# One 128-column product per pair of batches split into two 64-column products, one for each batch

## The chip, the cores and the metric

The kernel runs on one core of a Trainium2 chip. The time is the device time of one execution in microseconds (us). TensorE multiplies (a weight load, LDWEIGHTS, and then a matmul that streams the other operand's columns past it), VectorE and ScalarE read PSUM and write SBUF, GpSimd copies between places of SBUF, and SyncE issues most of the DMAs. The profile calls them PE (with PEld for the weight loads), DVE, ACT, POOL and SP.

## The reference, cut to what matters

64 batches of 64 tokens by 512 features go through four residual layers. The first two have a dense part and a low-rank adapter that is chosen per batch; the last two mix the 64 tokens of a batch with a 64 by 64 matrix chosen per batch.

```
x = x + x @ W_base.T + ((x @ Wt.T) @ A0[e0].T @ B0[e0].T) @ Wp.T * s0[e0]   # rank 16, 4 adapters
x = x + x @ W1.T + (x @ A1[e1].T) @ B1[e1].T * s1[e1]                       # rank 16, 8 adapters
x = x + einsum('bct,bcd->bdt', x, W2[e2])      # mixes tokens
x = x + einsum('bct,bcd->bdt', x, W3[e3])      # mixes tokens
```

## The kernel before

The first 48 us make tables out of the weights. With the identities added, the two dense layers become one 512 by 512 matrix G, kept as a high and a low part (`g01`, both in the 4-byte type fp32r, which the matmul reads at reduced precision; two parts win the precision back). The adapters become, for each adapter e, 16 columns U (`u_tab`, high and low part) and 16 rows V (`v_table`, in DRAM).

Then come 32 steps, one for each pair of batches, in 8 turns of 4 (`QUADS`, `QUAD`; the 6 turns in the middle are a hardware loop). A pair is 128 rows: 64 tokens of batch 0 and 64 of batch 1. TensorE does in one step (`step`, line 816):

- `mix` for the next pair: y = x^T times the token matrix, 4 full fp32 matmuls, which the profile shows as 8 records of 128 weight columns and 128 streamed columns. ScalarE copies the high part yh out of PSUM (`high_y`, line 402) and VectorE makes the low part yl (`low_y`, line 578), both into `yy`.
- z for this pair: 4 matmuls, one for each 128 of the 512 features. The weights are the 128 columns [Uh | Ul], 64 and 64, and each 64 are (batch 0, layer 1), (batch 0, layer 2), (batch 1, layer 1), (batch 1, layer 2) with 16 each. The streamed operand is [yh | yl] of both batches, 256 columns. Of the 128 by 256 results in `z_ps` only those are used where batch meets batch.
- in the third step of a turn (u = 2, seven times in all) `token_mix`, 16 records of 64 by 64, makes the token matrices of the next turn; ScalarE copies them (`copy_p`).
- o for this pair: 12 matmuls of yh and yl with G, 512 streamed columns, into one bank of `o_ps`, and behind them 2 matmuls with `z` as weights and V as streamed operand. Only these 2 wait for z.

Out of `z_ps` the kernel makes Uh·yh (rounded, to `z` rows 0 to 63: ScalarE, two instructions, one a batch), then its rounding rest plus Ul·yh plus Uh·yl (to `z` rows 64 to 127: `low_z` on VectorE, line 586, three stages of two instructions). `z` is zero where batch does not meet batch. ScalarE's order in a step is: z, (`copy_p` if u = 2), `high_y` of the next pair, `double_v` (line 421) of the next pair, `copy_out` (line 430) of this one. VectorE's is `low_z`, `low_y` of the next pair, and in the first two steps of a turn `add_w3` and `place_w2` (lines 606 and 621) for the next turn. GpSimd's `place_u` (line 313) fills `u_sel`, the weights of z, two steps ahead, once the z matmuls that read it are done. All engines run their orders as written and meet in semaphores: `z_done`, `zh_set`, `zl_set`, `yh_set`, `yl_set`, `o_done`, `o_set`.

Of the kernel before, what the change touches and what calls it, by code (L numbers as in the profile page):

```python
# [5 lines left out]
ALU = mybir.AluOpType  # L6
ACT = mybir.ActivationFunctionType
F32 = mybir.dt.float32
# [34 lines left out]
def build(nc, x, e0_ids, e1_ids, e2_ids, e3_ids, w_base, w_t, a0, b0, w_p, s0, w1, a1, b1, s1, w2, w3, out):  # L43
# [9 lines left out]
    with ctx:  # L53
        def sb(name, shape, dt=F32, of=ctx):
            return of.enter_context(nc.sbuf_tensor(name, shape, dt))

        def sem(name):
            return ctx.enter_context(nc.semaphore(name))
# [25 lines left out]

        wb_sb = sb("wb_sb", [PART, KC, D])
        wt_sb = sb("wt_sb", [PART, KC, D])
        u_sel = [sb(f"u_sel{n}", [PART, KC, 2, ZR], F32R) for n in range(2)]

        third = ExitStack()
        wpT = sb("wpT", [PART, 2, KC, D], F32R, of=third)  # L90
# [39 lines left out]
        w3_now = sb("w3_now", [PART, QUAD, SEQ])  # L130
        x_raw = sb("x_raw", [PART, QUAD, D])
        z = [sb(f"z{n}", [PART, PART], F32R) for n in range(2)]
        z_part = sb("z_part", [PART, 2, PART])

        v_sel = [sb(f"v_sel{u}", [PART, 2, D], F32R) for u in range(QUAD)]

# [29 lines left out]
        p_done, p_set = sem("p_done"), sem("p_set")  # L166
        x_in = [sem(f"x_in{h}") for h in range(2)]
        y_done, yh_set, yl_set = sem("y_done"), sem("yh_set"), sem("yl_set")
        z_rest, z_rest2 = sem("z_rest"), sem("z_rest2")
        u_placed = sem("u_placed")  # L170
        z_done, zh_set, zl_set = sem("z_done"), sem("zh_set"), sem("zl_set")
        v_in = [sem(f"v_in{u}") for u in range(QUAD)]
# [111 lines left out]
        @block.gpsimd  # L284
        def _(pool):

            nc.gpsimd.memset(ident[:, :], 0.0).then_inc(ones_set, 1)
            nc.gpsimd.iota(lane[:, :], pattern=[[0, PAIRS]], base=0, channel_multiplier=1).then_inc(iota_set, 1)
            nc.gpsimd.memset(owner[:, :], 1.0).then_inc(ones_set, 1)
            pool.wait_ge(ones_set, 2)  # L290
            nc.gpsimd.affine_select(out=ident[:, :], in_=ident[:, :], compare_op=ALU.not_equal, fill=1.0,  # L291
                                    base=0, pattern=[[-1, PART]], channel_multiplier=1).then_inc(ident_set, 1)

            nc.gpsimd.affine_select(out=owner[:, :], in_=owner[:, :], compare_op=ALU.is_ge, fill=0.0,
                                    base=0, pattern=[[-RANK, E1]], channel_multiplier=1).then_inc(ones_set, 1)
            pool.wait_ge(ones_set, 3)
            nc.gpsimd.affine_select(out=owner[:, :], in_=owner[:, :], compare_op=ALU.is_ge, fill=0.0,
                                    base=RANK - 1, pattern=[[RANK, E1]], channel_multiplier=-1).then_inc(ident_set, 1)

            for t in z:  # L300
                nc.gpsimd.memset(t[:, :].bitcast(F32), 0.0).then_inc(zero_set, 1)
            nc.gpsimd.memset(p_mix[:, :, :], 0.0).then_inc(zero_set, 1)

            def gather_w3(pairs):


                for j in pairs:
                    pool.indirect_dma_start(  # L308
                        out=w3_all[:, j, :], out_offset=None, in_=w3_flat,
                        in_offset=bass.IndirectOffsetOnAxis(ap=w3_rows[:, j:j + 1], axis=0)  # L310
                    ).then_inc(w3_in[min(j // QUAD, 2)], 16)

            def place_u(i, u):

                code = pool.value_load(ef_code[0:1, bass.ds(QUAD * i + u, 1)], min_val=0, max_val=(E0 * E1) ** 2 - 1)
                for b in range(2):
                    for part, e in ((0, (code >> (5 * b)) & (E0 - 1)), (1, ((code >> (5 * b + 2)) & (E1 - 1)) + E0)):
                        col = 32 * b + 16 * part
                        nc.gpsimd.tensor_copy(  # L319
                            u_sel[u % 2][:, :, :, col:col + RANK],  # L320
                            u_tab[:, :, :, bass.ds(e, 1), :].rearrange("p h k a r -> p k h (a r)")
                        ).then_inc(u_placed, 1)

            pool.wait_ge(rows_set, 1)
            gather_w3(range(0, QUAD))

            pool.wait_ge(wb_in, 16)
            for k in range(KC):
                blk = wb_sb[:, k, PART * k:PART * k + PART]
                nc.gpsimd.tensor_tensor(blk, blk, ident[:, :], ALU.add).then_inc(wb_plus, 1)  # L330
            for t in v_sel:
                nc.gpsimd.memset(t[:, 1, :].bitcast(F32), 0.0).then_inc(zero_set, 1)
            gather_w3(range(QUAD, 2 * QUAD))

            pool.wait_ge(code_set, 1)
            pool.wait_ge(setup_dve, DVE_DONE["u0"])
            for u in range(2):
                place_u(0, u)

            for i in range(QUADS):  # L340
                for u in range(QUAD):
                    if i < QUADS - 1 or u < 2:

                        pool.wait_ge(z_done, QUAD * i + u + 1)
                        place_u(i + (u + 2) // QUAD, (u + 2) % QUAD)
                    if i < QUADS - 2 and u == 1:
                        pool.wait_ge(w3_plus, i + 2)
                    if i < QUADS - 2 and u > 0:
                        gather_w3(range(QUAD * (i + 2) + u - 1, QUAD * (i + 2) + u + u // (QUAD - 1)))

        @block.scalar
        def _(act):
# [68 lines left out]
            def double_v(i, u):  # L421
# [5 lines left out]
                nc.scalar.activation(v_sel[u][ZR:, 0, :], v_sel[u][0:ZR, 0, :].bitcast(F32),  # L427
                                     ACT.Copy).then_inc(v_twice, 1)

            def copy_out(i, u):  # L430
                act.wait_ge(o_done, QUAD * i + u + 1)

                wait(act, o_out[u // 2], 16 * i)
                nc.scalar.activation(o_sb[:, u, :], o_ps[u % 2][:, :], ACT.Copy).then_inc(o_set, 1)  # L434

            def step(i, u, last):
                act.wait_ge(z_done, QUAD * i + u + 1)
                wait(act, o_done, QUAD * i + u - 1)
                for b in range(2):
                    rows, toks = slice(ZR // 2 * b, ZR // 2 * b + ZR // 2), slice(SEQ * b, SEQ * b + SEQ)  # L440
                    nc.scalar.activation(z[u % 2][rows, toks], z_ps[rows, toks], ACT.Copy).then_inc(zh_set, 1)  # L441
                if u == 2 and not last:
                    copy_p(i + 1)
                if not (last and u == QUAD - 1):
                    high_y(i, u + 1)
                if not (last and u == QUAD - 1):
                    double_v(i, u + 1)
                copy_out(i, u)
# [19 lines left out]
        def _(dve):  # L468
# [116 lines left out]

            def low_z(i, u):

                half = ZR // 2
                for b in range(2):
                    rows, toks = slice(half * b, half * b + half), slice(SEQ * b, SEQ * b + SEQ)  # L590
                    nc.vector.tensor_tensor(z_part[ZR + half * b:ZR + half * (b + 1), 0, toks], z_ps[rows, toks],  # L591
                                            z[u % 2][rows, toks].bitcast(F32), ALU.subtract).then_inc(z_rest, 1)
                for b in range(2):
                    rows, small = slice(half * b, half * b + half), slice(ZR + half * b, ZR + half * b + half)
                    toks = slice(SEQ * b, SEQ * b + SEQ)
                    dve.wait_ge(z_rest, 2 * (QUAD * i + u) + b + 1)
                    nc.vector.tensor_tensor(z_part[small, 1, toks], z_ps[small, toks], z_part[small, 0, toks],  # L597
                                            ALU.add).then_inc(z_rest2, 1)
                for b in range(2):
                    rows, small = slice(half * b, half * b + half), slice(ZR + half * b, ZR + half * b + half)  # L600
                    toks = slice(SEQ * b, SEQ * b + SEQ)
                    dve.wait_ge(z_rest2, 2 * (QUAD * i + u) + b + 1)
                    nc.vector.tensor_tensor(z[u % 2][small, toks], z_ps[rows, PART + SEQ * b:PART + SEQ * b + SEQ],  # L603
                                            z_part[small, 1, toks], ALU.add).then_inc(zl_set, 1)

            def add_w3(i):

# [23 lines left out]

            def turn(i, last=False):
                for u in range(QUAD):
                    dve.wait_ge(zh_set, 2 * (QUAD * i + u + 1))
                    low_z(i, u)
                    if not (last and u == QUAD - 1):
                        low_y(i, u + 1)
# [24 lines left out]
        def _(pe):  # L662
# [153 lines left out]
            def step(i, u, last):  # L816
# [6 lines left out]

                if u == 2 and not last:
                    token_ready(i + 1)
                wait(pe, zl_set, 2 * (QUAD * i + u))
                for k in range(KC):
                    done = mm(z_ps[:, 0:2 * PART], u_sel[n][:, k, :, :].rearrange("p h r -> p (h r)"),
                              yy[n][:, k, :, :].rearrange("p h t -> p (h t)"), k == 0, k == KC - 1)
                done.then_inc(z_done, 1)  # L830
                if u == 2 and not last:
                    token_mix(i + 1)
# [2 lines left out]
                for k in range(KC):  # L835
                    mm(o_ps[n][:, :], yy[n][:, k, 0, :], g01[:, 0, k, :], k == 0, False)
                    mm(o_ps[n][:, :], yy[n][:, k, 0, :], g01[:, 1, k, :], False, False)
                    mm(o_ps[n][:, :], yy[n][:, k, 1, :], g01[:, 0, k, :], False, False)

                pe.wait_ge(zl_set, 2 * (QUAD * i + u + 1))  # L840
                pe.wait_ge(v_twice, QUAD * i + u + 1)

# [43 lines left out]
```

## Time and profile before

| | us |
|---|---|
| median of 3 runs | 205.66 (205.35 to 206.56) |
| profiled execution, its own time | 204.97 |
| its span, first to last instruction | 201.8 |
| PE busy | 193.0 (96%) |
| PEld busy | 164.9 (82%) |
| DVE busy | 107.0 (53%) |
| ACT busy | 98.8 (49%) |

The span is what the trace covers; about 3.2 us of the execution's time lie around it. A busy PE is counted from the start of a matmul record to its end, and records overlap, so how fast TensorE goes is read from the distance between starts.

### The profile page before, as it was taken

To read this page: it belongs to the slowest core of one execution; us is meant where nothing else is said; L and a number is where in the kernel's file an instruction comes from. 1 tells how busy PE (TensorE), PEld (TensorE's weight loads), DVE (VectorE), ACT (ScalarE), POOL (GpSimd) and SP (SyncE) were. 2 spreads that over 40 slices of the span, in tenths; PEclk is the share of its full clock that TensorE was granted. 3 is DMA by queue.
4 is the path that set the end of the run, shared out by engine and by line. 5 is a ranking of instruction groups with operands and counts; after the bars stand their busy time and mean duration, and the time that the engine had idled before them with its cause. 6 is when DMAs were issued, how large, how long until landed. Compare 5 with 4: busy or idle time off the path is not lost.

```text
span 201.8 us, 5318 instructions
## 1 busy us (share of the span) xinstructions
PE 193.0 (96%) x1176; PEld 164.9 (82%) x1176; DVE 107.0 (53%) x348; ACT 98.8 (49%) x209; POOL 72.0 (36%) x181
## 2 busy tenths in 40 slices
PE   6779899998999999999999999999999999999993
PEld 6658687777888888888888888888888888888882
DVE  0366899743663475356445544763475347433351
ACT  2229484425545445445544555546545544555451
POOL 4425820031343534444452445243624352222200
PEclk9999999999999999999999999999999999999999
DMA  3979731912464637383755455564637373746322
GB/s 124 308 282 303 272 121 50 366 52 73 91 227 105 232 93 250 80 259 76 262 153 172 151 189 172 158 216 130 225 102 253 88 243 80 250 114 208 105 76 80
DMA packets 19903, 34.25 MB, mean 170 GB/s; under 512 B 6257, under 2 KB 6257, under 8 KB 19889
## 3 DMA queue, kind: packets, MB, share of 16 engines
q1 hardware_dynamic: 18864, 33.05, 51.3%
q0 software_dynamic: 1024, 1.05, 1.7%
q8 instruction: 4, 0.07, 0.1%
q14 instruction: 11, 0.08, 0.1%
HBM read 23.07 MB, written 11.01 MB: 169 GB/s over the span
## 4 chain that ended last, share of the span: by engine, by line
PE 90%; DMA 3%; DVE 3%; ACT 1%; SPq 1%; issue 1%; DVEq 0%
PE o_ps L675 53%; PE y_ps L675 17%; PE z_ps L675 9%; PE p_ps L675 5%; PE spare_ps L675 3%; DMA s_sb<-in_L_cond_scaling_dram 3%; DVE g L498 1%; DVE wpT L498 1%; PE spare_ps L687 0%; PE y_ps L754 0%; DVE b_by L492 0%; ACT g L355 0%; ACT o_sb L434 0%; PE z_ps L728 0%; ACT wpT L355 0%
## 5 line engine op out<-in xcount | busy, mean ns | idle before, releaser
L675 PE MATMUL o_ps<-g,yy 128*128 128x512 f32 x384 | 93.3, 392 | 0.0
L675 PEld LDWEIGHTS o_ps<-g,yy 128*128 128x128 f32 x384 | 69.8, 188 | 13.3
L319 POOL CAST u_sel<-u_tab 128x128 fp32r x128 | 34.1, 296 | 95.8 <-PE z_ps L675 70.6
L591 DVE TENSOR_TENSOR z_part<-z_ps,z 32x64 f32<-32x64 f32 x64 | 14.0, 218 | 59.8 <-ACT z L441 58.9
L434 ACT ACTIVATE o_sb<-o_ps 128x512 f32<-128x512 f32 x32 | 19.1, 598 | 45.6 <-PE o_ps L675 45.6
L308 POOL DMA_INDIRECT w_all<-in_L_cond_weights_dram,w_rows x32 | 31.9, 998 | 14.9 <-issue 10.9
L675 PEld LDWEIGHTS y_ps<-p_mix,x_raw 128*128 128x128 f32 x256 | 33.2, 191 | 3.4 <-DVE g L498 0.7
L675 PE MATMUL y_ps<-p_mix,x_raw 128*128 (+1 forms) x256 | 33.8, 275 | 0.5 <-DVE g L498 0.5
L441 ACT ACTIVATE z<-z_ps 32x64 fp32r<-32x64 f32 x64 | 13.7, 214 | 25.0 <-PE z_ps L675 24.2
L583 DVE TENSOR_TENSOR yy<-y_ps,yy 128x512 fp32r<-128x512 f32 x32 | 22.1, 692 | 3.0 <-ACT yy L407 2.1
L675 PE MATMUL z_ps<-yy,u_sel 128*128 128x256 f32 x128 | 22.9, 300 | 0.0
L427 ACT ACTIVATE v_sel<-v_sel 64x512 fp32r<-64x512 f32 x32 | 20.2, 631 | 0.8
L675 PE MATMUL o_ps<-v_sel,z 128*128 128x512 f32 x64 | 19.8, 390 | 0.0
L407 ACT ACTIVATE yy<-y_ps 128x512 fp32r<-128x512 f32 x32 | 19.2, 599 | 1.1 <-PE y_ps L675 0.4
L675 PEld LDWEIGHTS z_ps<-yy,u_sel 128*128 128x128 f32 x128 | 17.3, 190 | 0.1
L628 DVE COPY w_sel<-w2T 64x64 f32 x64 | 13.0, 203 | 6.1 <-issue 2.8
L597 DVE TENSOR_TENSOR z_part<-z_ps,z_part 32x64 f32<-32x64 f32 x64 | 14.4, 226 | 2.0
L603 DVE TENSOR_TENSOR z<-z_ps,z_part 32x64 fp32r<-32x64 f32 x64 | 14.0, 218 | 2.0
L675 PEld LDWEIGHTS o_ps<-v_sel,z 128*128 128x128 f32 x64 | 12.0, 188 | 2.4
L417 ACT ACTIVATE p_mix<-p_ps 64x256 f32 (+1 forms) x16 | 6.1, 379 | 2.8 <-PE p_ps L675 2.4
L701 PE MATMUL p_ps<-ident 128*128 128x128 f32 x36 | 5.6, 324 | 1.7 <-POOL ident L291 1.7
L701 PEld LDWEIGHTS p_ps<-ident 128*128 128x128 f32 x36 | 5.1, 169 | 1.7 <-POOL ident L291 1.7
(122 smaller groups left out, 138.0 us busy)
## 6 DMA issues: line engine op xcount, KB each, us to landing
x_raw<-in_x_dram SPq DMA_DIRECT2D x16, 512.0 KB, 3.4
v_sel<-v_table SPq DMA_DIRECT2D x128, 64.0 KB, 2.1
out_dram<-o_sb SPq DMA_DIRECT2D x14, 512.0 KB, 3.1
v_table<-t_parts SPq DMA_DIRECT2D x4, 512.0 KB, 3.6
wp_sb<-in_L_cond_Wp_dram SPq DMA_DIRECT2D x2, 512.0 KB, 4.6
w_sb<-in_L_cond_W_dram SPq DMA_DIRECT2D x1, 1024.0 KB, 8.0
wb_sb<-in_L_cond_W_base_dram SPq DMA_DIRECT2D x1, 1024.0 KB, 10.8
wt_sb<-in_L_cond_Wt_dram SPq DMA_DIRECT2D x1, 1024.0 KB, 7.6
```

Source lines behind the costliest of these rows:

```text
L308: pool.indirect_dma_start(out=w3_all[:, j, :], out_offset=None, in_=w3_flat, in_offset=bass.IndirectOffsetOnAxis(ap=w3_rows[:, j:j + 1], a ...
L319: nc.gpsimd.tensor_copy(u_sel[u % 2][:, :, :, col:col + RANK], u_tab[:, :, :, bass.ds(e, 1), :].rearrange("p h k a r -> p k h (a r)")).the ...
L407: nc.scalar.activation(yy[u % 2][:, :, 0, :], y_ps[u % 2][:, :].rearrange("p (k t) -> p k t", k=KC), ACT.Copy).then_inc(yh_set, 1)
L427: nc.scalar.activation(v_sel[u][ZR:, 0, :], v_sel[u][0:ZR, 0, :].bitcast(F32), ACT.Copy).then_inc(v_twice, 1)
L434: nc.scalar.activation(o_sb[:, u, :], o_ps[u % 2][:, :], ACT.Copy).then_inc(o_set, 1)
L441: nc.scalar.activation(z[u % 2][rows, toks], z_ps[rows, toks], ACT.Copy).then_inc(zh_set, 1)
L583: nc.vector.tensor_tensor(yy[u % 2][:, :, 1, :], y_ps[u % 2][:, :].rearrange("p (k t) -> p k t", k=KC), yy[u % 2][:, :, 0, :].bitcast(F32) ...
L591: nc.vector.tensor_tensor(z_part[ZR + half * b:ZR + half * (b + 1), 0, toks], z_ps[rows, toks], z[u % 2][rows, toks].bitcast(F32), ALU.sub ...
L597: nc.vector.tensor_tensor(z_part[small, 1, toks], z_ps[small, toks], z_part[small, 0, toks], ALU.add).then_inc(z_rest2, 1)
L603: nc.vector.tensor_tensor(z[u % 2][small, toks], z_ps[rows, PART + SEQ * b:PART + SEQ * b + SEQ], z_part[small, 1, toks], ALU.add).then_in ...
L628: nc.vector.tensor_copy(w2_sel[rows, u, :], w2T[rows, bass.ds(g, 1), :].rearrange("p a c -> p (a c)")).then_inc(w2_placed, 1)
L675: return nc.tensor.matmul(dst, lhsT, rhs, start=start, stop=stop)
```

## The change

z is made batch by batch: for each of the two batches 4 matmuls, whose weights are the 64 columns [Uh | Ul] of that batch (32 and 32) and whose streamed operand is the 128 columns [yh | yl] of that batch. They write 64 rows of `z_ps` in place of 128. `place_u` writes the same number of elements to other places. Since high and low U of both batches now stand in the same rows, the parts are added for both batches at once on 32 rows by 128 columns: ScalarE moves Ul·yh to rows 0 to 31; VectorE adds Uh·yl, then Uh·yh; ScalarE rounds the sum; then ScalarE copies the rounded sum to `z` rows 0 to 63 (two instructions) and VectorE writes the rest to `z` rows 64 to 127 (two instructions). The z matmuls wait for the sum of the step before in place of its `zl_set`, and the last two o matmuls wait for `zh_set` too.

```diff
-        u_sel = [sb(f"u_sel{n}", [PART, KC, 2, ZR], F32R) for n in range(2)]
+        u_sel = [sb(f"u_sel{n}", [PART, KC, 2, 2, ZR // 2], F32R) for n in range(2)]
...
+            def high_z(i, u):
+                act.wait_ge(z_done, QUAD * i + u + 1)
+                low_u = z_ps[ZR // 2:ZR, 0:2 * PART].rearrange("p (b h t) -> p b h t", b=2, h=2)[:, :, 0]
+                nc.scalar.activation(z_part[:, 0, :, :], low_u, ACT.Copy).then_inc(z_moved, 1)
+                act.wait_ge(z_sum, QUAD * i + u + 1)
+                nc.scalar.activation(z_part[:, 3, :, :].bitcast(F32R), z_part[:, 2, :, :], ACT.Copy).then_inc(z_round, 1)
+                wait(act, o_done, QUAD * i + u - 1)
+                act.wait_ge(z_round, QUAD * i + u + 1)
+                for b in range(2):
+                    rows, toks = slice(ZR // 2 * b, ZR // 2 * b + ZR // 2), slice(SEQ * b, SEQ * b + SEQ)
+                    nc.scalar.activation(z[u % 2][rows, toks], z_part[:, 3, b, :], ACT.Copy).then_inc(zh_set, 1)
...
             def low_z(i, u):
+                high_u = z_ps[0:ZR // 2, 0:2 * PART].rearrange("p (b h t) -> p b h t", b=2, h=2)
+                dve.wait_ge(z_moved, QUAD * i + u + 1)
+                nc.vector.tensor_tensor(z_part[:, 1, :, :], high_u[:, :, 1], z_part[:, 0, :, :],
+                                        ALU.add).then_inc(z_part_sum, 1)
+                dve.wait_ge(z_part_sum, QUAD * i + u + 1)
+                wait(dve, zh_set, 2 * (QUAD * i + u))
+                nc.vector.tensor_tensor(z_part[:, 2, :, :], high_u[:, :, 0], z_part[:, 1, :, :],
+                                        ALU.add).then_inc(z_sum, 1)
+                dve.wait_ge(z_round, QUAD * i + u + 1)
+                wait(dve, o_done, QUAD * i + u - 1)
+                for b in range(2):
+                    small = slice(ZR + ZR // 2 * b, ZR + ZR // 2 * b + ZR // 2)
+                    nc.vector.tensor_tensor(z[u % 2][small, SEQ * b:SEQ * b + SEQ], z_part[:, 2, b, :],
+                                            z_part[:, 3, b, :], ALU.subtract).then_inc(zl_set, 1)
...
-                wait(pe, zl_set, 2 * (QUAD * i + u))
-                for k in range(KC):
-                    done = mm(z_ps[:, 0:2 * PART], u_sel[n][:, k, :, :].rearrange("p h r -> p (h r)"),
-                              yy[n][:, k, :, :].rearrange("p h t -> p (h t)"), k == 0, k == KC - 1)
+                wait(pe, z_sum, QUAD * i + u)
+                for b in range(2):
+                    for k in range(KC):
+                        done = mm(z_ps[0:ZR, PART * b:PART * b + PART],
+                                  u_sel[n][:, k, b, :, :].rearrange("p h r -> p (h r)"),
+                                  yy[n][:, k, :, SEQ * b:SEQ * b + SEQ], k == 0, k == KC - 1)
...
+                pe.wait_ge(zh_set, 2 * (QUAD * i + u + 1))
                 pe.wait_ge(zl_set, 2 * (QUAD * i + u + 1))
                 pe.wait_ge(v_twice, QUAD * i + u + 1)
```

## Rows read from the trace of the kernel before

**Rows 1.** The page: busy time of three engines; granted TensorE clock in slices.
```profile
PE 193.0 (96%) x1176; PEld 164.9 (82%) x1176; DVE 107.0 (53%) x348; ACT 98.8 (49%) x209; POOL 72.0 (36%) x181
...
PEclk9999999999999999999999999999999999999999
```
**Rows 2.** Chain of waits: start us, us, what (one token step's z, one plain step).
```profile
96.00 0.52 PE z_ps L675 x4
...
100.51 0.89 PE y_ps L675 x8
101.40 0.47 PE z_ps L675 x4
101.87 3.19 PE o_ps L675 x14
```
**Rows 3.** Instruction groups by shape: busy us, mean ns | idle before, releaser.
```profile
L583 DVE TENSOR_TENSOR yy<-y_ps,yy 128x512 fp32r<-128x512 f32 x32 | 22.1, 692 | 3.0 <-ACT yy L407 2.1
L427 ACT ACTIVATE v_sel<-v_sel 64x512 fp32r<-64x512 f32 x32 | 20.2, 631 | 0.8
...
L434 ACT ACTIVATE o_sb<-o_ps 128x512 f32<-128x512 f32 x32 | 19.1, 598 | 45.6 <-PE o_ps L675 45.6
...
L675 PEld LDWEIGHTS z_ps<-yy,u_sel 128*128 128x128 f32 x128 | 17.3, 190 | 0.1
...
L591 DVE TENSOR_TENSOR z_part<-z_ps,z 32x64 f32<-32x64 f32 x64 | 14.0, 218 | 59.8 <-ACT z L441 58.9
L441 ACT ACTIVATE z<-z_ps 32x64 fp32r<-32x64 f32 x64 | 13.7, 214 | 25.0 <-PE z_ps L675 24.2
...
L675 PEld LDWEIGHTS p_ps<-wt,a0T 128*64 128x64 f32 x12 | 1.6, 135 | 1.0
```
**Rows 4.** Timeline of PE and PEld: start us, us, engine, what, count.
```profile
18.51 0.19 PEld L675 LDWEIGHTS spare_ps<-v0T,a1T 128*128 128x128 f32 x1 [0.43 <-ACT g L355]
18.54 0.27 PE L675 MATMUL spare_ps<-v0T,a1T 128*128 128x64 f32 x1 [0.22 <-DVE v0T L498]
...
18.54 1.50 PE L675 MATMUL spare_ps<-v0T,a1T 128*128 128x64 f32 x12 [0.22 <-DVE v0T L498]
...
20.54 0.35 PE L687 MATMUL o_ps<-ident,a_sb 64*128 64x64 f32 x3
...
42.83 0.34 PE L675 MATMUL p_ps<-w_now,w_sel 64*64 64x64 f32 x6
...
47.53 0.19 PEld L675 LDWEIGHTS y_ps<-p_mix,x_raw 128*128 128x128 f32 x1 [0.71 <-DVE g L498]
47.53 0.38 PE L675 MATMUL y_ps<-p_mix,x_raw 128*128 128x128 f32 x1 [0.52 <-DVE g L498]
```
**Rows 5.** Timeline of PE in a token step.
```profile
95.82 0.71 PE L675 MATMUL z_ps<-yy,u_sel 128*128 128x256 f32 x4
96.45 0.68 PE L675 MATMUL p_ps<-w_now,w_sel 64*64 64x64 f32 x16
```
**Rows 6.** Timeline of all engines, from z to the last o matmuls of a plain step.
```profile
101.16 0.72 PE L675 MATMUL z_ps<-yy,u_sel 128*128 128x256 f32 x4
...
101.91 0.46 ACT L441 ACTIVATE z<-z_ps 32x64 fp32r<-32x64 f32 x2 [0.77 <-PE z_ps L675]
...
102.40 0.47 DVE L591 TENSOR_TENSOR z_part<-z_ps,z 32x64 f32<-32x64 f32 x2 [2.87 <-ACT z L441]
...
103.41 0.47 DVE L603 TENSOR_TENSOR z<-z_ps,z_part 32x64 fp32r<-32x64 f32 x2
...
104.22 0.41 PEld L675 LDWEIGHTS o_ps<-v_sel,z 128*128 128x128 f32 x2
...
105.10 0.60 ACT L434 ACTIVATE o_sb<-o_ps 128x512 f32<-128x512 f32 x1 [1.46 <-PE o_ps L675]
```
**Rows 7.** Timeline of DVE in the first step of a turn and after.
```profile
90.56 1.05 DVE L628 COPY w_sel<-w2T 64x64 f32 x4
92.45 0.47 DVE L591 TENSOR_TENSOR z_part<-z_ps,z 32x64 f32<-32x64 f32 x2 [0.84 <-ACT z L441]
```

More of the change, by code:

```diff
@@ L132, in build @@
         z = [sb(f"z{n}", [PART, PART], F32R) for n in range(2)]
-        z_part = sb("z_part", [PART, 2, PART])
+        z_part = sb("z_part", [ZR // 2, 4, 2, SEQ])
         v_sel = [sb(f"v_sel{u}", [PART, 2, D], F32R) for u in range(QUAD)]
@@ L168, in build @@
         y_done, yh_set, yl_set = sem("y_done"), sem("yh_set"), sem("yl_set")
-        z_rest, z_rest2 = sem("z_rest"), sem("z_rest2")
+        z_moved, z_part_sum, z_sum, z_round = sem("z_moved"), sem("z_part_sum"), sem("z_sum"), sem("z_round")
         u_placed = sem("u_placed")
@@ L317, in place_u @@
                     for part, e in ((0, (code >> (5 * b)) & (E0 - 1)), (1, ((code >> (5 * b + 2)) & (E1 - 1)) + E0)):
-                        col = 32 * b + 16 * part
                         nc.gpsimd.tensor_copy(
-                            u_sel[u % 2][:, :, :, col:col + RANK],
+                            u_sel[u % 2][:, :, b, :, RANK * part:RANK * part + RANK],
                             u_tab[:, :, :, bass.ds(e, 1), :].rearrange("p h k a r -> p k h (a r)")
@@ L436, in step @@
             def step(i, u, last):
[L437 to L441, printed above, removed]
+                high_z(i, u)
                 if u == 2 and not last:
@@ L586, in low_z @@
             def low_z(i, u):
-                half = ZR // 2
-                for b in range(2):
[L590 to L604, printed above, removed]
+                high_u = z_ps[0:ZR // 2, 0:2 * PART].rearrange("p (b h t) -> p b h t", b=2, h=2)
@@ L633, in turn @@
                 for u in range(QUAD):
-                    dve.wait_ge(zh_set, 2 * (QUAD * i + u + 1))
                     low_z(i, u)
```

## The prediction

> **What bounds the kernel now.** The page first: PE is busy for 193.0 of 201.8 us, DVE for 107.0 and ACT for 98.8, and the granted clock is at 9 or more tenths in every slice, the upper of its two levels, 2.4 GHz [rows 1]. Then the chain of waits: from 47.5 us to the end it never leaves TensorE but for the last copy out, and each step is the same three pieces, y 0.89, z 0.47, o 3.19 us, together 4.55 [rows 2]. Nothing on another engine ends last, so the change is worth what it does to TensorE's own z piece, unless it makes z so late that the last two o matmuls wait. The 4 z matmuls of a token step (u = 2, seven of the 32 steps) take 0.52 in the chain [rows 2].
>
> **What sets the distance of two matmuls.** Two things can: streaming the columns of one, and loading the weights of the next beside it. The end of a lone matmul, counted from the start of its load, is load + stream + a fixed tail. The first y matmul (fp32) starts with its load at 47.53 and ends 0.38 later; the first of the twelve fp32r matmuls with 128 weight columns and only 64 streamed ones has its load at 18.51 and ends at 18.81, 0.30 later [rows 4]. The loads are alike (0.19), so that one's stream is 0.08 shorter. The y one's stream can be no longer than the distance of two of them, 0.89/8 = 0.111 [rows 2] (128 columns at half a column per tick of 2.4 GHz are 0.107), so 64 fp32r columns take at most 0.03 us: one column a tick, even in a short fp32r matmul. The z ones of now, 256 columns, stand (0.47/4 =) 0.117 apart, the o ones, 512 columns, 3.19/14 = 0.228 [rows 2]; 256 more columns cost 0.111, so 128 fewer cost 0.055 less, and the z matmuls of 128 columns should stand 0.062 apart as far as streaming goes.
> The load: a record with 64 weight columns is 135 ns long, one with 128 is 190, so 64 columns fewer save 55 ns [rows 3]. The twelve short matmuls with 128 weight columns stand (1.50 - 0.28)/11 = 0.111 apart although each streams for only 0.03 [rows 4]: that is the time of a 128-column load. A 64-column load is then 0.111 - 0.055 = 0.056, a little under the 0.062 of the stream. Between seven of the new z matmuls and the next, the distance is 0.062. Bounds from rows: the 64-column flips with 128-by-64 weights, which stream at half speed and so as long as 128 fp32r columns, stand (0.35 - 0.22)/2 = 0.063 apart; six 64 by 64 records that run in pairs, side by side, span 0.34 - 0.22 = 0.12 for two distances, 0.058 with the 6 ns inside a pair taken off [rows 4]. I take 0.062, between 0.058 and 0.063.
> At the end of the group stands the catch: behind the eighth z matmul comes the first o matmul, whose 128 weight columns need 0.111 to load, and the eighth streams for only 0.053. Today the fourth z matmul streams for 0.107 and hides it.
>
> **The change part by part.**
> 1. z on TensorE, plain step: from 0.47 to 7 x 0.062 + 0.111 = 0.545, that is +0.075 (ends: 7 x 0.058 + 0.111 = 0.517, +0.047; 7 x 0.063 + 0.111 = 0.552, +0.082). The streamed columns are as many as before, 4 x 256 = 8 x 128: that half of the weight columns goes saves no time, because columns of weights are not what TensorE streams. 25 plain steps: +1.9 us (+1.2 to +2.1).
> 2. z in a token step. Now 0.52, because three more waits put the first z load later, and its 128 columns no longer fit beside the last y matmul; half as many fit, which gives the 0.05 back. The matmul behind z is a 64-row one that starts 0.20 after the start of the fourth z matmul (96.53 - 0.28 = 96.25, against 96.45) [rows 5]: it waits for the stream (0.107) and for about 0.1 more; behind the new eighth it starts at 0.15. From the fourth's start on that is 0.05 less, while the three distances before (3 x 0.117 = 0.35) become seven (7 x 0.062 = 0.43): +0.08 - 0.05 - 0.05 = -0.02, ends -0.05 and +0.03. Seven steps: -0.15 us (-0.35 to +0.2).
> 3. One more wait ahead of the last two o matmuls: the weight load behind it has 0.22 of streaming beside it and needs 0.111, so some 0.05 of issuing stays hidden. If z came late it would cost all of its lateness, which is the next point.
> 4. The way from z_done to a full `z`. Now: ACT starts at 101.91, the last DVE instruction ends at 103.88, 1.97 later; the load of `z` as weights starts at 104.22, 0.34 behind that [rows 6]. After: an instruction of 128 elements on DVE costs 218 + 64 x (692 - 218)/448 = 286 ns, on ACT from PSUM 214 + 64 x (598 - 214)/448 = 269, on ACT from SBUF 33 more (631 against 598 at 512 elements), so 302, and with 64 elements 247 [rows 3]. A hand-over is 0.03 (ACT ends at 102.37, DVE starts at 102.40 [rows 6]); I take 0.04 for five of them, the waits of an engine on itself among them. Sum: move 0.27, add 0.29, add 0.29, round 0.30, two copies to `z` 0.49, hand-overs 0.20 = 1.84. DVE's two subtractions run beside ACT's two copies and are shorter. What is allowed: z_done comes earlier against the o group, since the last z matmul streams 0.053 in place of 0.107 and the o matmul follows at 0.111 in place of 0.117, so the load is due 2.31 + 0.05 = 2.36 behind ACT's start, and another 0.11 can be lost before TensorE stands. Slack 0.5 to 0.6 us. Cost nothing (bounds: no gain, since nothing waited; for a loss see the second rival).
> 5. ACT's queue. The three stages that wait for DVE stand in ACT's one queue, ahead of `copy_p`, `high_y` of the next pair, `double_v` and `copy_out`. `high_y` starts 1.84 + 0.03 behind ACT's start in place of 0.48, so 1.4 later. `copy_out` of now waits 1.46 for o [rows 6], and takes that shift just so; it is late by at most 0.1, and its reader on TensorE is two steps on. `low_y` is late too: it ends at about 101.91 + 1.87 + 0.60 + 0.03 + 0.69 = 105.10, and the next z load is due 4.55 behind the last, at 105.7: 0.6 left. In a token step 0.78 of `copy_p` more comes between, in a step that is 0.8 longer: the same.
> 6. DVE loses two small instructions and two halves, in all 6 x 0.22 becomes 2 x 0.29 + 2 x 0.21, some 0.3 a step. In the first step of a turn it ends its `place_w2` at 91.61 and is wanted at 92.45 [rows 7]; there `low_y` starts 0.5 later and so do these; its next instruction is due at about 92.3, so 0.2 is left, and behind it the 0.5 of point 4. Cost nothing. GpSimd writes as much as before, `z_done` frees its buffers within 0.03 of today, and SP's queue has no new wait.
>
> Sum: +1.9 - 0.15 = +1.7 us. The profiled execution would go from 204.97 to 206.7; it lies 0.7 under the median of the runs, so against 205.66 the forecast is 207.3. Its own range, from the ends of points 1 and 2, is +0.9 to +2.2: 206.6 to 207.9.
>
> **The rivals.**
> - *The load behind the eighth z matmul is hidden after all* (not slower). If the load of a 128-column block can begin while two short matmuls are still to stream, the last distance is 0.06 too: 8 x 0.058 to 8 x 0.062 = 0.46 to 0.50, -0.01 to +0.03 in a plain step, and in token steps point 2's -0.15 us stays. Time 205.2 to 206.2. It decides as soon as the first o matmul starts within 0.08 of the eighth z. For it: nothing in the trace shows a short stream followed by a longer load. Against: in the twelve short matmuls each load starts only when the one before is through, 0.111 apart [rows 4]. Chance 0.2.
> - *The new chain to z is late* (slower by more). It takes 0.5 more than I work out: if an instruction on 32 partitions with an engine's wait for itself cost 0.1 more at each of five places, or DVE is late in the first step of a turn. Each 0.1 us beyond the slack costs 3.2 us over 32 steps, 0.8 if only the first steps of turns are hit. Time 208 to 211. For it: four changes of engine where there was one. Against: the chain worked out is shorter than today's, which has 0.34 to spare. Chance 0.1.
> - *A pair of a load and a short matmul has a floor above 0.062.* The nearest row from above is 0.111, the distance of pairs with 128 weight columns; with that, 8 x 0.111 = 0.89, +0.42 in a plain step, +0.38 in a token step, some +13 us, 219. From below it is the forecast. Against: the flips at 0.063 and the paired records are loads and matmuls too [rows 4]. I put it at 208 to 213, with a chance of 0.06. The Trainium skill, TensorE: Matmul & The Clock Gate, section Back-to-back issue gap, speaks against this change: it states about 81 ns a matmul for a stream of load and matmul pairs of 128 streamed columns. By that the z piece would be 7 x 0.081 + 0.111 = 0.68, +0.21, an estimate of 211 for the kernel from that page. The trace has no single-stream pair of just this shape, but its flips at 0.063 do not keep to that floor.
> - *Short fp32r matmuls stream slower than a column a tick.* At half speed 8 x 0.111, 219 again; at a quarter 8 x 0.22 = 1.8, +1.3 x 32, 248. The lone short matmul above ends 0.08 too early for a quarter. Chance 0.03.
>
> **How the numbers follow.** Forecast 0.58 (207.3); hidden load 0.2; late chain 0.1; floor 0.06; slow stream 0.03; something I can't name that makes it faster by over 0.5% 0.03. About 0.5% (1.03 us: 204.6 to 206.7) is what a measurement of this kernel can tell from no change. The hidden load is "same" (0.18) or a little faster (0.02), and the low end of the forecast, with the scatter of a median, puts 0.09 of its 0.58 there too. So faster 0.03 + 0.02 = 0.05, same 0.18 + 0.09 = 0.27, slower 0.49 + 0.1 + 0.06 + 0.03 = 0.68. The range reaches from the middle of the hidden-load case to the lower part of the late chain: 205.6 to 208.9.
>
> **What would show it.** In the changed kernel's timeline: z matmuls 0.06 apart, the first o matmul 0.11 behind the eighth; the chain's z piece at 0.54 and y and o as now; `z` ready some 0.5 ahead of its load; ACT's wait before `copy_out` gone from 1.46 to near 0; no PE piece in the chain broken by DVE or ACT. Wrong, if the chain goes over ACT or DVE within the steps, if the last distance is 0.06, or if the z matmuls stand more than 0.07 apart.

## The result and the profile after

The changed kernel takes 211.34 us (median of 6, 209.97 to 212.54) against 205.76 (6 runs, 205.12 to 207.34): ratio 1.0255, 95% interval 1.0202 to 1.0309. It is slower, as forecast, but by 5.6 us and not by 1.7, and above the range of 205.6 to 208.9. (Ratios are estimated from the fast runs alone, so they are not exactly the quotients of the medians.) The profiled execution took 209.97 us with a span of 207.8.

First the page of the changed kernel: busy time of the engines, the chain's shares, and the groups that answer to [rows 1, 3].

```profile
PE 196.1 (94%) x1304; PEld 166.9 (80%) x1304; DVE 97.0 (47%) x284; ACT 120.0 (58%) x273; POOL 71.7 (35%) x181
...
PE 62%; DVE 10%; ACT 9%; issue 8%; DVEq 5%; DMA 3%; SPq 1%; ACTq 1%
...
L593 DVE TENSOR_TENSOR yy<-y_ps,yy 128x512 fp32r<-128x512 f32 x32 | 22.1, 692 | 28.2 <-ACT yy L406 28.2
...
L683 PE MATMUL z_ps<-yy,u_sel 128*64 128x128 f32 x256 | 22.8, 232 | 2.6 <-DVE w_sel L637 2.5
...
L683 PEld LDWEIGHTS z_ps<-yy,u_sel 128*64 128x64 f32 x256 | 19.1, 136 | 4.2 <-issue 3.7
...
L448 ACT ACTIVATE o_sb<-o_ps 128x512 f32<-128x512 f32 x32 | 19.1, 597 | 3.2 <-PE o_ps L683 1.7
```

VectorE's work is 10 us less and ScalarE's 21 us more. What matters stands elsewhere: `low_y` (L593) now waits 28.2 us in all for ScalarE's `high_y` (L406), where it waited 2.1 [rows 3]; `copy_out` waits 1.7 for o in place of 45.6; and for the first time TensorE stands in the steps, 2.5 us by the PE row and 4.2 by the row of the weight loads.

The chain of waits says where. One turn of it, from the step after a token mix to the next token step (start us, us, what):

```profile
102.98 0.89 PE y_ps L683 x8
103.87 0.48 PE z_ps L683 x8
104.36 3.25 PE o_ps L683 x14
107.60 0.89 PE y_ps L683 x8
108.49 0.50 PE z_ps L683 x8
109.02 0.28 ACT z_part L433
109.31 0.29 DVE z_part L600
109.72 0.29 DVE z_part L605
110.03 0.32 ACT z_part L436
110.77 0.21 ACT z L442
111.00 0.61 ACT yy L406
...
114.13 0.29 DVE z_part L600
114.53 0.29 DVE z_part L605
114.85 0.32 ACT z_part L436
115.58 0.23 issue
115.81 0.61 ACT yy L406
117.90 0.23 issue
118.12 0.66 PE z_ps L683 x8
```

A plain step is 0.89 + 0.48 + 3.25 = 4.62 us where it was 4.55 [rows 2]. In the first two steps of a turn the chain leaves TensorE: move, two additions, rounding, copy to `z`, `high_y` (L406), and the same once more. The timeline of the second step and of the start of the third shows what comes behind `high_y` (all engines; lines of PE's long pieces, POOL and SP left out).

```profile
113.04 1.05 DVE L637 COPY w_sel<-w2T 64x64 f32 x4 [0.39 <-issue]
...
113.64 0.27 ACT L433 ACTIVATE z_part<-z_ps 32x128 f32<-32x128 f32 x1 [0.70 <-PE z_ps L683]
114.13 0.28 DVE L600 TENSOR_TENSOR z_part<-z_ps,z_part 32x128 f32<-32x128 f32 x1
114.53 0.28 DVE L605 TENSOR_TENSOR z_part<-z_ps,z_part 32x128 f32<-32x128 f32 x1
...
114.85 0.31 ACT L436 ACTIVATE z_part<-z_part 32x128 fp32r<-32x128 f32 x1 [0.94 <-DVE z_part L605]
115.19 0.47 DVE L612 TENSOR_TENSOR z<-z_part 32x64 fp32r<-32x64 f32 x2 [0.38 <-ACT z_part L436]
115.25 0.54 ACT L442 ACTIVATE z<-z_part 32x64 fp32r<-32x64 f32 x2
115.81 0.60 ACT L406 ACTIVATE yy<-y_ps 128x512 fp32r<-128x512 f32 x1
...
116.00 0.41 PEld L683 LDWEIGHTS o_ps<-v_sel,z 128*128 128x128 f32 x2
...
116.44 0.69 DVE L593 TENSOR_TENSOR yy<-y_ps,yy 128x512 fp32r<-128x512 f32 x1 [0.79 <-ACT yy L406]
...
117.05 0.84 DVE L637 COPY w_sel<-w2T 64x64 f32 x4
...
118.09 0.55 PEld L683 LDWEIGHTS z_ps<-yy,u_sel 128*64 128x64 f32 x8 [0.55 <-issue]
118.12 0.66 PE L683 MATMUL z_ps<-yy,u_sel 128*64 128x128 f32 x8 [0.39 <-DVE w_sel L637]
```

`high_y` ends at 116.41, `low_y` at 117.13, `place_w2` (L637) at 117.89, and the z load that waits for it (`token_ready`) starts at 118.09. TensorE has been free since about 117.56 (its last y matmul started at 116.68 + 1.05 - 0.28 = 117.45 and streams for 0.11). `z` itself is ready at 115.79, 0.2 ahead of its load at 116.00: it is not the one that is late, though in the loop's first turn only 0.05 is left at this place. In the first, third and fourth steps of a turn it is ready 0.4 or more ahead.

Beside it the same place in the kernel before, which the prediction did not look at. The placing ends at 114.50 and the z load starts at 114.78: there was no slack to begin with.

```profile
113.61 0.89 DVE L628 COPY w_sel<-w2T 64x64 f32 x4
...
114.78 0.54 PEld L675 LDWEIGHTS z_ps<-yy,u_sel 128*128 128x128 f32 x4
```

From here on two measures are used: the median of the runs, and, inside the trace, the distance from the start of the first z matmul to the start of the last. The second leaves out the setup, whose length differed from one profiled execution to the next (first z matmul 48.4 to 51.3 us after the start), though its code is the same in all of them. It is 146.6 us before and 152.3 after, +5.6 before rounding. This measure is the steadier one, for a second reason: part of an execution's time lies around the span. That part is 1.7 to 2.3 us in nearly all runs of the changed kernels, but in those of the kernel before it is 1.9 to 2.3 in some and 2.9 to 3.5 in others, so a median can differ from its neighbour by half a microsecond or more for a reason that is not in the kernel's steps.

### The profile page after: what moved, and what is told of

Read it like the earlier page. It is cut to its first block, busy times and chain, and to the rows that moved or that the text cites. A ratio compares the mean times of both kernels' runs of the same rounds, so it can differ in the third digit from the quotient of the medians.

```text
span 207.8 us, 5575 instructions
## 1 busy us (share of the span) xinstructions
PE 196.1 (94%) x1304; PEld 166.9 (80%) x1304; DVE 97.0 (47%) x284; ACT 120.0 (58%) x273; POOL 71.7 (35%) x181
## 3 DMA queue, kind: packets, MB, share of 16 engines
q0 software_dynamic: 1024, 1.05, 1.7%
## 4 chain that ended last, share of the span: by engine, by line
PE 62%; DVE 10%; ACT 9%; issue 8%; DVEq 5%; DMA 3%; SPq 1%; ACTq 1%
PE o_ps L683 32%; PE y_ps L683 11%; PE z_ps L683 8%; PE p_ps L683 5%; ACT yy L406 4%; DMA s_sb<-in_L_cond_scaling_dram 3%; PE spare_ps L683 3%; DVEq L637 3%; DVE w_sel L637 3%; ACT z_part L436 2%; DVE z_part L605 2%; DVE z_part L600 2%; DVE g L508 1%; DVEq L628 1%; ACT z L442 1%
## 5 line engine op out<-in xcount | busy, mean ns | idle before, releaser
L683 PE MATMUL o_ps<-g,yy 128*128 128x512 f32 x384 | 94.9, 396 | 0.0
L308 POOL DMA_INDIRECT w_all<-in_L_cond_weights_dram,w_rows x32 | 31.4, 980 | 15.9 <-issue 11.0
L593 DVE TENSOR_TENSOR yy<-y_ps,yy 128x512 fp32r<-128x512 f32 x32 | 22.1, 692 | 28.2 <-ACT yy L406 28.2
L600 DVE TENSOR_TENSOR z_part<-z_ps,z_part 32x128 f32<-32x128 f32 x32 | 8.9, 279 | 36.9 <-ACT z_part L433 36.8
L683 PE MATMUL z_ps<-yy,u_sel 128*64 128x128 f32 x256 | 22.8, 232 | 2.6 <-DVE w_sel L637 2.5
L436 ACT ACTIVATE z_part<-z_part 32x128 fp32r<-32x128 f32 x32 | 9.9, 310 | 24.6 <-DVE z_part L605 24.6
L433 ACT ACTIVATE z_part<-z_ps 32x128 f32<-32x128 f32 x32 | 8.6, 268 | 25.9 <-PE z_ps L683 25.7
L683 PEld LDWEIGHTS z_ps<-yy,u_sel 128*64 128x64 f32 x256 | 19.1, 136 | 4.2 <-issue 3.7
L612 DVE TENSOR_TENSOR z<-z_part 32x64 fp32r<-32x64 f32 x64 | 15.7, 246 | 13.6 <-ACT z_part L436 12.6
L406 ACT ACTIVATE yy<-y_ps 128x512 fp32r<-128x512 f32 x32 | 19.1, 598 | 1.1 <-PE y_ps L683 0.4
L442 ACT ACTIVATE z<-z_part 32x64 fp32r<-32x64 f32 x64 | 16.4, 256 | 3.6
L637 DVE COPY w_sel<-w2T 64x64 f32 x64 | 12.0, 188 | 6.1 <-issue 2.7
L605 DVE TENSOR_TENSOR z_part<-z_ps,z_part 32x128 f32<-32x128 f32 x32 | 8.9, 279 | 3.4
(124 smaller groups left out, 149.1 us busy)
```

The lines of the kernel that those rows point to most:

```text
L308: pool.indirect_dma_start(out=w3_all[:, j, :], out_offset=None, in_=w3_flat, in_offset=bass.IndirectOffsetOnAxis(ap=w3_rows[:, j:j + 1], a ...
L406: nc.scalar.activation(yy[u % 2][:, :, 0, :], y_ps[u % 2][:, :].rearrange("p (k t) -> p k t", k=KC), ACT.Copy).then_inc(yh_set, 1)
L436: nc.scalar.activation(z_part[:, 3, :, :].bitcast(F32R), z_part[:, 2, :, :], ACT.Copy).then_inc(z_round, 1)
L442: nc.scalar.activation(z[u % 2][rows, toks], z_part[:, 3, b, :], ACT.Copy).then_inc(zh_set, 1)
L593: nc.vector.tensor_tensor(yy[u % 2][:, :, 1, :], y_ps[u % 2][:, :].rearrange("p (k t) -> p k t", k=KC), yy[u % 2][:, :, 0, :].bitcast(F32) ...
L600: nc.vector.tensor_tensor(z_part[:, 1, :, :], high_u[:, :, 1], z_part[:, 0, :, :], ALU.add).then_inc(z_part_sum, 1)
```

## Experiments

**1. The short matmuls alone.** The kernel before with the changed z matmuls and the changed `u_sel`, and its own evacuation.

```diff
-                for k in range(KC):
-                    done = mm(z_ps[:, 0:2 * PART], u_sel[n][:, k, :, :]..., yy[n][:, k, :, :]..., k == 0, k == KC - 1)
+                for b in range(2):
+                    for k in range(KC):
+                        done = mm(z_ps[0:ZR, PART * b:PART * b + PART], u_sel[n][:, k, b, :, :]...,
+                                  yy[n][:, k, :, SEQ * b:SEQ * b + SEQ], k == 0, k == KC - 1)
```

> The kernel before with the eight short z matmuls alone (64 weight columns, 128 streamed) and its own chain of ScalarE and VectorE instructions, in number, shape and order as before; these read rows of z_ps that the short matmuls don't write, so what is added to the output for the adapters is not the reference's. Theory A: this part alone costs what the plain steps show, 0.073 a step, and nothing waits: 205.7 + 1.6 = 207.3 (207.0 to 207.7), each first o matmul's record 0.05 longer than before. Theory C: 211. If short matmuls cost nothing and all of the loss is waiting: 205.7.

Measured: ratio 1.0048 (0.9998 to 1.0097), median 206.38 against 205.57; first to last z 148.2 us, +1.6. Every plain step is 4.62 and no load of z waits. The runs' scatter hides whether it is +0.8 or +1.6; the trace, whose plain steps mostly repeat to 0.01, says 1.6. The median lies 0.6 below the expected 207.0 to 207.7. So of the 5.6 us the short matmuls are 1.6, and 4.1 (from unrounded numbers) come with the new chain.

**2. The new chain alone.** The changed kernel with the four wide z matmuls.

```diff
-                for b in range(2):
-                    for k in range(KC):
-                        done = mm(z_ps[0:ZR, PART * b:PART * b + PART], ...)
+                for k in range(KC):
+                    done = mm(z_ps[:, 0:2 * PART], ..., k == 0, k == KC - 1)
```

> The changed kernel with the four wide z matmuls of the kernel before (and their layout of u_sel), so only the new chain of ScalarE and VectorE is left; it adds up other parts of z_ps than belong together, so the adapters' part of the output is not the reference's. Theory A (stall in the third step of a turn, 0.62 a turn, from the late place_w2, whatever the z matmuls are): 205.7 + 4.0 = 209.7 (209.2 to 210.2). Theory C (short matmuls are the whole loss): 205.7. Theory B (the new z is late for the last two o matmuls): 211 with TensorE idle ahead of them.

Measured: ratio 1.0222 (1.0152 to 1.0293), median 210.5, above the expected 209.2 to 210.2. Plain steps are at 4.55 again, and the loss stands ahead of z in the third step of all seven turns (weight loads of z; in brackets the idle time before):

```profile
118.21 0.53 PEld L683 LDWEIGHTS z_ps<-yy,u_sel 128*128 128x128 f32 x4 [0.69 <-issue]
137.98 0.53 PEld L683 LDWEIGHTS z_ps<-yy,u_sel 128*128 128x128 f32 x4 [0.66 <-issue]
```

It is more than the 4.0 expected, because with steps 0.07 shorter the same chain is later still: from the third turn on z starts 0.76 to 0.82 behind the last y matmul in the third steps, where it is 0.64 to 0.67 in the changed kernel, and two steps 0.07 shorter account for that difference. The two parts of the change therefore don't add: alone they cost 1.6 and 5.4 from first to last z, together 5.6.

**3. Let TensorE wait later.** The changed kernel with the wait for the placed matrices ahead of the eighth z matmul.

```diff
-                if u == 2 and not last:
-                    token_ready(i + 1)
...
+                        if b == 1 and k == KC - 1 and u == 2 and not last:
+                            token_ready(i + 1)
                         done = mm(z_ps[0:ZR, ...
```

> The changed kernel, with one thing moved: in the third step of a turn TensorE waits for the next turn's placed matrices (token_ready) only ahead of the eighth z matmul, not ahead of the first. Theory A (the z matmuls of the third step stand because VectorE's place_w2 of the second step is late; about 0.62 us a turn, seven turns, 4.3 us of the 5.6): the wait shrinks to 0.62 - 0.43 = 0.1 to 0.2 a turn, so 3 us less than the changed kernel's 211.3: 208.0 to 208.6. Theory B (the chain from z_done to a full z is late, and TensorE waits there): nothing changes, 211.3. Theory C (the loss is spread evenly over the z matmuls, because short matmuls are slow): 211.3.

Measured: 207.45 (ratio 1.0109, 1.0064 to 1.0154), 3.9 less than the changed kernel by the medians, 3.1 less (149.1) from first to last z, which is the 3 expected. In six of the seven third steps the first load of z doesn't wait, and what is left behind it is 0.09 us or less. In the second turn, the first of the loop, 0.4 is left: z starts 0.2 late there, 0.25 behind the end of `low_y`. The median is better than the expected 208.0 to 208.6, and theories B and C fall: neither a late `z` nor slow short matmuls would have moved.

**4. Place earlier.** The changed kernel with `place_w2` of the second step ahead of `low_y` on VectorE.

```diff
                     low_z(i, u)
+                    if u == 1 and not last:
+                        place_w2(i + 1, code, range(2, 4))
                     if not (last and u == QUAD - 1):
                         low_y(i, u + 1)
```

> The changed kernel, with one thing moved on VectorE: in the second step of a turn place_w2 stands ahead of low_y of the next pair, in the 0.79 us in which VectorE now waits for ScalarE's high_y. Theory A (late place_w2): the matrices are there some 0.7 earlier, the stall of 0.62 a turn goes, 4 us less: 207.3 (206.9 to 207.8). low_y may end 0.2 later, in front of a z matmul due 0.4 behind it. Theory B or C: 211.3.

Measured: 209.89 (ratio 1.0196, 1.0092 to 1.0300). A miss: 1.4 of the 4 us came back by the medians, whose interval does not tell it from none, and 0.7 from first to last z (151.5). The matrices are there in time now, and still z waits (VectorE and the loads of z around the third step):

```profile
115.31 0.92 DVE L637 COPY w_sel<-w2T 64x64 f32 x4
...
116.27 0.69 DVE L593 TENSOR_TENSOR yy<-y_ps,yy 128x512 fp32r<-128x512 f32 x1
...
117.47 0.55 PEld L684 LDWEIGHTS z_ps<-yy,u_sel 128*64 128x64 f32 x8 [0.29 <-issue]
```

Placing ends at 116.23, but `low_y`, whose result z needs too, ends at 116.96, and the z load starts 0.5 behind that. In between TensorE issues the five waits that stand behind the one for `low_y` (for `u_sel`, three in `token_ready`, and for the old `z_ps`). The trace has their control instructions, which the views leave out, at 117.00, 117.10, 117.20, 117.30 and 117.39. When the wait ahead of them is released late, there is nothing for these 0.5 us to hide behind.

**5. Both moves.**

> The changed kernel with both moves: place_w2 of the second step ahead of low_y on VectorE, and token_ready ahead of the eighth z matmul on TensorE. Each move alone left something (place_early 209.9, late_ready 207.5). Theory A2: behind the late place_w2 a second thing is late, yl_set, and between yl_set and the first z load of the third step stand five wait instructions of about 0.1 us each; with token_ready moved only three are left and the matrices are there long before, so nothing is left of the stall: 147.8 us from the first to the last z as in mm_only, 206.4 to 207.0. Rival: low_y itself is too late for z (its own 0.2 to 0.3 behind place_w2): TensorE still stands 0.2 or more a turn ahead of the first z matmul, 208 or more.

Measured: 207.61 (ratio 1.0135, 1.0059 to 1.0212), first to last z 149.4. Theory A2 missed by more than half a microsecond, and the rival's 208 was not reached either. Two of the seven turns have no stall, the others one of 0.07 to 0.5 us, the longest:

```profile
78.20 0.55 PEld L684 LDWEIGHTS z_ps<-yy,u_sel 128*64 128x64 f32 x8 [0.41 <-issue]
```

So fewer waits do not settle it; with the placing in front of it `low_y` is itself late in most turns, as the rival said: wherever TensorE stands, the load starts 0.21 behind the end of `low_y`. What makes it late stands on ScalarE.

**6. `high_y` into ScalarE's own gap.** The changed kernel with `high_y` of the next pair between the move and the rounding, where ScalarE waits mostly 0.75 us, in the second steps 0.94, for VectorE's two additions.

```diff
                 nc.scalar.activation(z_part[:, 0, :, :], low_u, ACT.Copy).then_inc(z_moved, 1)
+                if not (last and u == QUAD - 1):
+                    high_y(i, u + 1)
                 act.wait_ge(z_sum, QUAD * i + u + 1)
...
                 high_z(i, u)
...
-                if not (last and u == QUAD - 1):
-                    high_y(i, u + 1)
```

> The changed kernel, with one thing moved on ScalarE: high_y of the next pair stands between the move of Ul*yh and the rounding, where ScalarE waits for VectorE's two additions. Theory A, in full (place_w2 is late because low_y waits for high_y, and that stands behind the new stages that wait for VectorE): low_y starts about as early as in the kernel before, the stall in the third step goes, 207.3 (206.9 to 207.8). If place_w2 is late for another reason (the register work ahead of it, the first step's add_w3): 210 to 211.3. Theory B: high_y (0.60) is longer than the gap that it fills by some 0.1, so z is as late or later: 211.3 or more.

Measured: 206.47 against 205.57, ratio 1.0013 (0.9971 to 1.0055); first to last z 148.2 us, the same as with the short matmuls alone, and no z starts more than 0.04 us late in a third step. The median lies 0.4 below the expected range, as that of the short matmuls did. The timeline of a plain step shows the gap filled: `high_y` ends at 107.76, 0.1 ahead of the second addition (107.86), so it fits and the rounding waits only for the addition; and `low_y` starts right behind VectorE's part of `z` (second fence: `low_y` of the step before, whose `z` ended at 104.14).

```profile
106.87 0.27 ACT L433 ACTIVATE z_part<-z_ps 32x128 f32<-32x128 f32 x1 [0.77 <-PE z_ps L683]
107.16 0.60 ACT L406 ACTIVATE yy<-y_ps 128x512 fp32r<-128x512 f32 x1
...
107.58 0.28 DVE L605 TENSOR_TENSOR z_part<-z_ps,z_part 32x128 f32<-32x128 f32 x1
107.89 0.31 ACT L438 ACTIVATE z_part<-z_part 32x128 fp32r<-32x128 f32 x1
```
```profile
104.17 0.69 DVE L593 TENSOR_TENSOR yy<-y_ps,yy 128x512 fp32r<-128x512 f32 x1
```

One instruction moved on ScalarE gives all 4.1 us of the chain back (152.3 to 148.2): this is the cause, and experiments 3 to 5 treated its effects. 0.2 of it is in no third step but at the very end. The last pair has no y matmuls between the o group and its z to hide behind, and in the changed kernel TensorE stands there for `low_y`:

```profile
199.99 0.69 DVE L593 TENSOR_TENSOR yy<-y_ps,yy 128x512 fp32r<-128x512 f32 x1 [0.78 <-ACT yy L406]
...
200.74 0.55 PEld L683 LDWEIGHTS z_ps<-yy,u_sel 128*64 128x64 f32 x8 [0.48 <-DVE yy L593]
```

**7. The same wait without the change.** The kernel before with a delay on VectorE ahead of the second step's `place_w2`.

```diff
+                    if u == 1 and not last:
+                        for n in range(2):
+                            nc.vector.tensor_tensor(t0_sum[:, n, :], v0g1[:, :], gu1T[:, :], ALU.add)
                     if u < 2 and not last:
                         place_w2(i + 1, code, range(2 * u, 2 * u + 2))
```

> The kernel before, with two additions of 128 by 512 on scratch added on VectorE ahead of place_w2 in the second step of each turn: a delay of about 1.3 us there and nowhere else, the z matmuls and their chain untouched. Theory A (the third step's z waits for place_w2 and has some 0.3 of slack): TensorE stands 1.3 - 0.3 = 1.0 a turn ahead of the first z matmul of the third step, seven turns: 205.7 + 7 = 212.7 (211.5 to 213.5). If VectorE has the slack that its 53% of busy time suggests, or the wait is elsewhere: 205.7.

Measured: 212.44 (ratio 1.0322, 1.0262 to 1.0382), as expected. TensorE stands ahead of z in every turn:

```profile
121.72 0.54 PEld L678 LDWEIGHTS z_ps<-yy,u_sel 128*128 128x128 f32 x4 [1.01 <-issue]
```

The placing now ends 1.96 us behind `low_y`, where it ended 0.76 to 0.94 behind it, so the delay is 1.0 to 1.2 us and not 1.3, and nearly all of it becomes stall: the 0.3 of slack that the expectation granted is not there. All this on an engine that is busy half of the time.

**8. The load behind the eighth matmul.** Experiment 3 with the eighth z matmul twice as wide.

```diff
+                        wide = b == 1 and k == KC - 1
-                        done = mm(z_ps[0:ZR, PART * b:PART * b + PART], ..., yy[n][:, k, :, SEQ * b:SEQ * b + SEQ], ...)
+                        done = mm(z_ps[0:ZR, 2 * PART:4 * PART] if wide else ..., yy[n][:, k, :, :]... if wide else ..., ...)
```

> late_ready with the eighth z matmul streaming 256 columns in place of 128, into columns of z_ps that nobody reads (so one quarter of the second batch's z is left out). If the load of the first o matmul's 128 weight columns is what TensorE waits for behind the eighth z matmul (0.111 of load beside 0.053 of stream), the 128 columns more fill the time that is lost anyway: the same time as late_ready within 0.3 us, and the first o matmul's record shrinks from 0.447 to 0.397. If streaming is what counts in the whole group, 0.055 more in each of 32 steps: 1.8 us over late_ready.

Measured: 208.07 (ratio 1.0130, 1.0064 to 1.0197) against 207.45 for experiment 3, which the intervals don't tell apart. The trace does: plain steps are 4.62 in both, with 128 columns more in one of them, and the first o matmul's record is 0.397 long in place of 0.447. In token steps, where the next load is a small one, the columns cost 0.10 (first to last z 149.9 against 149.1). The exposed load is what TensorE loses in a plain step.

**9. The wait moved in the kernel before.** The kernel before, with `token_ready` ahead of the fourth of its four z matmuls.

```diff
-                if u == 2 and not last:
-                    token_ready(i + 1)
...
                 for k in range(KC):
+                    if k == KC - 1 and u == 2 and not last:
+                        token_ready(i + 1)
                     done = mm(z_ps[:, 0:2 * PART], ...
```

> The kernel before, with token_ready moved from ahead of the first to ahead of the fourth z matmul. In the kernel before, the first z matmul of the third step starts 0.03 to 0.13 behind the last y matmul, where other steps have 0.03; four of seven turns show 0.06 to 0.10 of delay. If that is all that the wait costs there: 0.3 us faster at most, 205.4, not to be told from 205.7. If it has a larger hidden cost: 204.7 or less.

Measured: 204.55 against 205.49, ratio 0.9968 (0.9934 to 1.0001). It was repeated:

> The kernel before with token_ready ahead of the fourth z matmul, once more, to narrow the interval of 0.9934 to 1.0001. If the 0.33 us that its trace is shorter between the first and the last z is all: ratio 0.9984. If the first measurement was right: 0.9968.

Measured: 204.14 against 205.54, ratio 0.9944 (0.9913 to 0.9976). Both traces are 0.3 us shorter from first to last z (146.3): the third step's z starts 0.03 behind the last y in every turn, where it was up to 0.13. The medians show 0.9 and 1.4 us, but this is not all the kernel's doing. On average the runs that enter the ratio have 2.0 us around the span in this version, both times, and 2.6 in the kernel before, where some have about 3. The spans themselves differ by +0.15 us in the first measurement and -0.5 in the second. So 0.3 us is what the traces bear out; why the time around the span differs is open.

## Why the prediction was wrong

- *What bounds the kernel, and the arithmetic of matmuls*: right. z matmuls stand 0.061 apart (0.062 forecast), a short fp32r matmul streams a column a tick, and the load behind the eighth is not hidden: the first o matmul's record grew from 0.397 to 0.447. It shows there and not in the z piece (0.48), so two of the forecast's signs were wrong: "z piece at 0.54", and "the first o matmul 0.11 behind the eighth". It starts 0.06 behind, which was to be the sign of the rival that the load is hidden. By that sign alone one would have chosen the wrong theory; the record's length and experiment 8 decide. z and o together are 3.73 against 3.66. That is +0.073 a plain step (+0.075 forecast) and +0.02 in a token step (-0.02), 1.9 us in all when nothing waits (148.2 in experiment 1 against 146.3 in experiment 9). Measured against the kernel before it is +1.6 (+1.7 forecast), because the 0.3 us that z of the third steps waited there goes away with the longer steps. That the two agree to 0.1 is in part luck.
- *Point 4, z in time*: right in its verdict. The chain took 109.02 to 110.98, 1.96 us against 1.84: VectorE's second addition starts 0.13 behind the end of the first, the copies to `z` 0.09 behind the rounding, where 0.04 each was put, and the copies take 0.54, not 0.49. In the second steps of the loop's turns it took 2.13 to 2.15 (2.41 once), since VectorE was still placing, and the forecast 0.5 ahead of the load became 0.2.
- *Point 5, "cost nothing"*: `high_y` was 1.5 us later in a plain step (1.4 forecast) and 1.7 in the second step, and `low_y` ended 0.3 ahead of the due z load (117.13 against 112.84 + 4.62 = 117.46) and not 0.6. The point took the load's due time for the time by which its operand must be there; in the third step five waits of 0.1 us stand between. In the changed kernel this costs 0.2 us, at the last pair; it is what spoiled experiments 4 and 5.
- *Point 6, "cost nothing"*: this is the step that failed, by 4 us. It followed the late `low_y` to `place_w2` in the first step only and asked whether VectorE would be free again (it was not: the addition started 0.2 late, 113.90 to 114.13). It did not ask who waits for the placed matrices: `token_ready`, in TensorE's own queue, for the second step's. That wait had no slack in the kernel before (114.50 to 114.78, and in five turns of seven z started 0.07 to 0.13 behind the last y where other steps have 0.03, which point 2 put down to issuing alone). A shift of 0.76 us of the placing, from 3.49 behind ScalarE's first z instruction (111.01 to 114.50) to 4.25 (113.64 to 117.89), became 0.6 of stall a turn.
- *The rivals*: the late chain was the nearest (208 to 211, chance 0.1), but named the wrong place. `z` was never late; its chain held up the work queued behind it. The Trainium skill's 81 ns a matmul (TensorE: Matmul & The Clock Gate, Back-to-back issue gap) gave an estimate of 211 too (211.7 with its token steps counted); the trace disagrees with it, with a median of 61 ns over 224 distances. The floor rival's own 208 to 213 holds the measured time as well, and falls by the same distances. A time that comes out right proves no mechanism.

## What to carry to other kernels

An engine at half load can be one that everything waits for: when an instruction becomes late, follow every instruction queued behind it to the semaphore that it sets, and every waiter of that, step by step through the whole period and not only in the step that looks tightest. A chain that goes to and fro between two engines holds both queues; put the next independent instruction (here `high_y`, 0.60 us) into the gap (here 0.75) in which the engine would wait. And fewer weight columns gain nothing where the streamed columns set the time; a short stream ahead of a wide load even loses the part of the load that it can't cover.

## What the runs showed of the hardware that was not expected

- A wait that is released late costs more than its lateness: in the third step z's load started 0.20 us after the last placing in the changed kernel and 0.5 after `low_y` in experiment 4, the time of two and of five wait instructions.
- An instruction that waits for the one before it on VectorE started 0.13 us after its end in the 24 steps of the hardware loop (0.41 between starts of 0.28 us instructions), but 0.03 after it in the 8 steps outside the loop, as a hand-over to ScalarE does. Operands and shapes are the same. In the loop the trace has one control instruction more between the two additions (at 114.44, on the line of the `wait` helper, whose value there depends on the loop counter). That it makes the difference is likely, but no run tests it. Lines of a step outside the loop, to be set beside 114.13 and 114.53 above:

```profile
197.78 0.28 DVE L600 TENSOR_TENSOR z_part<-z_ps,z_part 32x128 f32<-32x128 f32 x1 [1.71 <-ACT z_part L433]
198.09 0.28 DVE L605 TENSOR_TENSOR z_part<-z_ps,z_part 32x128 f32<-32x128 f32 x1
```
